# Writing out the batch loop, and reworking the first microseconds and the last stages, of a scan-mixer kernel

## The reference

```python
# mixer block, on u = layernorm(x)
logits  = u @ gate_W                          # 4 mixers, the best 2 per token are used
weights = softmax(top2(logits))
g, v, d = u @ Wg[m] + bg, u @ Wv[m] + bv, u @ Wd[m] + bd      # m = 0..3, each 256 -> 256
h[m]    = linear_scan(sigmoid(g) * tanh(v), 0.001 + 0.998 * sigmoid(d))   # along the 1024 tokens
a       = sum over the chosen m of weight[m] * h[m]
t       = x + layernorm(a)
# expert block, on z = layernorm(layernorm(t)) * ln_g + ln_b
e, gate = argmax and max of softmax(batchnorm(mean over tokens of z) @ Wr + br)   # one expert of 8 per sequence
y       = (relu(z @ W_down[e] + b_down[e]) @ W_up[e] + b_up[e]) * gate            # 256 -> 64 -> 256
out     = t + layernorm(y)
```

## Time and profile before

| | us |
|---|---|
| median of 3 runs (lowest, highest) | 683.45 (683.26, 683.74) |
| the profiled execution's own time | 683.75 |
| its span, from the first instruction to the last | 681.9 |
| PE (TensorE matmul) busy | 624.9, 92% |
| DVE (VectorE) busy | 595.3, 87% |
| ACT (ScalarE) busy | 432.1, 63% |
| POOL (GpSimd) busy | 162.8, 24% |

### The profile page before, as it was taken

The page is one execution under the profiler, slowest core; times in us unless marked ns, Lnnn a source line. Parts: engine busy times, 40 slices in busy tenths (PEclk is TensorE's granted clock), DMA queues, the critical chain, the costliest instruction groups (busy, mean ns, idle before and its releaser), DMA issues. The chain is left out here.

```text
span 681.9 us, 11013 instructions
## 1 busy us (share of the span) xinstructions
PE 624.9 (92%) x3457; PEld 331.8 (49%) x3457; DVE 595.3 (87%) x1289; ACT 432.1 (63%) x757; POOL 162.8 (24%) x238
## 2 busy tenths in 40 slices
PE   3999989999999999999999999999999999999132
PEld 1555445555545554555545554555545554554121
DVE  7593999979999899989999899989999889978976
ACT  2757746875578657775578657875678655776033
POOL 2006024101820065101820064102720051101111
PEclk9999998999999999999999999999999999999666
DMA  8800522030312113030313023030311010000003
GB/s 230 206 1 0 124 91 65 2 105 1 124 32 69 37 65 93 1 105 1 124 31 81 25 72 87 1 105 1 124 31 43 1 63 2 0 13 1 0 26 110
DMA packets 63702, 39.08 MB, mean 57 GB/s; under 512 B 34934, under 2 KB 63642, under 8 KB 63642
## 3 DMA queue, kind: packets, MB, share of 16 engines
q1 hardware_dynamic: 63644, 38.34, 20.3%
HBM read 21.03 MB, written 8.39 MB: 43 GB/s over the span
## 5 line engine op out<-in xcount | busy, mean ns | idle before, releaser
L1229 PE MATMUL ps_main<-x_feat,w_hi 128*128 128x512 f16 x1536 | 471.3, 381 | 2.4 <-ACT x_feat L541 1.5
L1229 PE MATMUL ps_main<-x_feat,w_lo 128*128 128x512 f16 x768 | 292.4, 381 | 0.0
L1229 PEld LDWEIGHTS ps_main<-x_feat,w_hi 128*128 128x128 f16 x1536 | 151.6, 99 | 179.8 <-issue 3.1
L837 DVE TENSOR_TENSOR_SCAN hid<-decay_s,value_s 128x1024 f32<-128x1024 f32 (+1 forms) x64 | 144.7, 2260 | 6.7 <-DVE value_s L857 1.7
L562 ACT ACTIVATE value_s<-ps_main,vecs 128x512 f32<-128x512 f32 x128 | 88.6, 692 | 90.0 <-PE ps_main L1229 89.9
L562 ACT ACTIVATE decay_s<-ps_main,vecs 128x512 f32<-128x512 f32 x128 | 88.6, 692 | 62.5 <-PE ps_main L1229 50.5
L1229 PEld LDWEIGHTS ps_main<-x_feat,w_lo 128*128 128x128 f16 x768 | 75.5, 98 | 83.8 <-issue 1.4
L562 ACT ACTIVATE gate_s<-ps_main,vecs 128x512 f32<-128x512 f32 x128 | 88.6, 692 | 42.0 <-PE ps_main L1229 39.8
L447 POOL TENSOR_TENSOR root_y<-root_in_y,neg_half 128x8 f32<-128x8 f32 (+1 forms) x9 | 18.8, 2091 | 292.1 <-DVE root_in_y L943 292.1
L850 DVE SCALAR_TENSOR_TENSOR mixed<-ps_aux,comb,mixed 128x256 f32<-128x256 f32 x192 | 77.2, 474 | 12.1 <-PE ps_aux L1239 9.9
L857 DVE TENSOR_TENSOR value_s<-gate_s,value_s 128x1024 f32<-128x1024 f32 (+1 forms) x66 | 78.3, 1187 | 5.7 <-ACT value_s L562 5.7
(11 more groups left out here) (158 smaller groups left out, 548.4 us busy)
## 6 DMA issues: line engine op xcount, KB each, us to landing
x_in<-in_L_attn_x SPq DMA_DIRECT2D x16, 512.0 KB, 4.4
resid<-in_L_attn_x SPq DMA_DIRECT2D x7, 1024.0 KB, 5.2
out<-resid SPq DMA_DIRECT2D x7, 1024.0 KB, 4.5
expert<-experts SPq DMA_DIRECT2D x8, 192.5 KB, 2.2
w_stage<-in_L_attn_Wg SPq DMA_DIRECT2D x4, 256.0 KB, 3.8
w_stage<-in_L_attn_Wd SPq DMA_DIRECT2D x4, 256.0 KB, 5.1
w_stage<-in_L_attn_Wv SPq DMA_DIRECT2D x4, 256.0 KB, 5.1
u_split<-in_L_ffn_W_down SPq DMA_DIRECT2D x4, 256.0 KB
```

What stands on the lines that cost most here:

```text
L837: dve.tensor_tensor_scan(states(pc), staged(decay_s, pc, pc.c), staged(value_s, pc, pc.c), start, ALU.mult, ALU.add).then_inc(scanned, 1)
L1229: ins = pe.matmul(ps_main[:, i % BANKS], w[:, 3 * m + kind, k, half * P:(half + 1) * P], feat(low, bt, k, c), start=(n == 0), stop=(n == 3 ...
```

## The change

Every engine's stream is written out: the `Fori` loops become Python loops, and semaphore increments that nobody waited for go (`plain_begun`, `turn_begun`, `index_seen`, `shift_begun`). TensorE's stream now begins with 45 transposes of the identity into a PSUM bank, whose result is never read. The first bank's six matmuls are reordered, high x first, and each waits for its own input. W_down is loaded once, in two DMAs instead of four, and `hidden_bias` takes two experts per matmul (eight instead of sixteen), whose sums VectorE adds in four pieces instead of one. In batch 7's last stages TensorE gets 16, 8, 15, 2 and 2 matmuls of 128x512 whose result is never read (`keep_awake`), `down` is replaced by `down_last` (six matmuls of 64 output rows per chunk instead of four of 128), `join_h` and `low_h` by `plain_h` with ScalarE on one side of chunk 1, and the last rows are shared: ScalarE scales 6 tiles, VectorE scales 2 and adds 6, GpSimd adds 2.

```diff
-            with eng.Fori(0, B // 2 - 1) as j:
+            for j in range(B // 2 - 1):
...
-            for k in range(KT):
-                for a in range(2):
-                    sp.dma_start(down_stage[:, :, k, a * H:(a + 1) * H],
-                                 W_down[:, k * P:(k + 1) * P, :].rearrange("e p h -> p e h")
-                                 ).then_inc(experts_loaded, 16)
+            for k in range(KT):
+                sp.dma_start(down_stage[:, k], W_down[:, k * P:(k + 1) * P, :].rearrange("e p h -> p e h")
+                             ).then_inc(experts_loaded, 16)
...
-                for part in range(2 * C):
-                    sp.wait_ge(out_ready, C * bt.n + part + 1)
+                for part, ready, count in ((0, early_out, 1), (1, out_ready, C * bt.n + 1), (3, own_out, 1),
+                                           (2, out_ready, C * bt.n + 2)):
+                    sp.wait_ge(ready, count)
...
+                rows = t_rows(bt)
+                for t in scalar_rows(0)[:T // C // 2]:
+                    pool.wait_ge(y_normed, T + t + 1)
+                    ins = pool.tensor_tensor(rows[:, t], y_rows[:, t], rows[:, t], ALU.add)
+                ins.then_inc(early_out, 1)
...
                 router_sigmoids(bt)
-                for c in range(C):
-                    hidden_part(bt, c)
-                    high_h(bt, c)
+                act.wait_ge(h_ready, done(bt, 0))
+                act.activation(up_in2[0:H, chunk(0)], h32[0:H, chunk(0)], ACT.Relu).then_inc(hp_ready, 1)
+                act.wait_ge(down_done, done(bt, 1))
+                act.activation(h32[0:H, chunk(1)], ps_aux[0:H, KT], ACT.Relu,
+                               bias=expert[0:H, HB:HB + 2].bitcast(F32), scale=Q_W * H_SCALE).then_inc(hh_ready, 1)
+                act.wait_ge(hh_ready, done(bt, 0))
+                act.activation(up_in1[0:H, chunk(1)], h32[0:H, chunk(1)], ACT.Copy).then_inc(hh_ready, 1)
+                act.activation(up_in2[0:H, chunk(1)], h32[0:H, chunk(1)], ACT.Copy).then_inc(hp_ready, 1)
                 for c in range(C):
                     act.wait_ge(y_scaled, B + c)
-                    scale_rows(tiles(c))
+                    scale_rows(scalar_rows(c))
...
+            def plain_h(b, c):
+                if c == 0:
+                    dve.wait_ge(down_done, done(b, c))
+                    dve.tensor_scalar(h32[0:H, chunk(c)], ps_aux[0:H, KT * c], Q_W * H_SCALE,
+                                      expert[0:H, HB:HB + 2].bitcast(F32), ALU.mult, ALU.add).then_inc(h_ready, 1)
+                    dve.wait_ge(h_ready, done(b, c))
+                    dve.tensor_scalar(up_in1[0:H, chunk(c)], h32[0:H, chunk(c)], 0.0, None, ALU.max
+                                      ).then_inc(h_rounded, 1)
+                    dve.wait_ge(h_rounded, 1)
+                else:
+                    dve.wait_ge(hh_ready, done(b, c))
+                dve.scalar_tensor_tensor(up_in1[H:P, chunk(c)], h32[0:H, chunk(c)], 0.0, up_in1[0:H, chunk(c)],
+                                         ALU.max, ALU.subtract).then_inc(up_in_ready, 1)
+            def finish_last(b):
+                rows = t_rows(b)
+                own = [t for t in tiles(1) if t not in scalar_rows(1)]
+                dve.wait_ge(y_scaled, b.n + C)
+                for t in own:
+                    dve.tensor_scalar(y_rows[:, t], ps_tok[:, t], mul_by["y"][:, t:t + 1], add_y[:, t:t + 1],
+                                      ALU.mult, ALU.add).then_inc(own_rows, 1)
+                for n, t in enumerate(scalar_rows(0)[T // C // 2:]):
+                    dve.wait_ge(y_normed, T + T // C // 2 + n + 1)
+                    ins = dve.tensor_tensor(rows[:, t], y_rows[:, t], rows[:, t], ALU.add)
+                ins.then_inc(out_ready, 1)
+                for n, t in enumerate(own):
+                    dve.wait_ge(own_rows, n + 1)
+                    ins = dve.tensor_tensor(rows[:, t], y_rows[:, t], rows[:, t], ALU.add)
+                ins.then_inc(own_out, 1)
+                for n, t in enumerate(scalar_rows(1)):
+                    dve.wait_ge(y_normed, T + T // C + n + 1)
+                    ins = dve.tensor_tensor(rows[:, t], y_rows[:, t], rows[:, t], ALU.add)
+                ins.then_inc(out_ready, 1)
...
+                early = first and pc.plane == 0 and kind == GATE
...
+                terms = [(k, w, low) for k in range(KT) for w, low in ((w_hi, 0), (w_lo, 0), (w_hi, 1))]
+                if early:
+                    terms.sort(key=lambda term: term[2])
+                for n, (k, w, low) in enumerate(terms):
+                    if early:
+                        pe.wait_ge(xl_ready if low else xh_ready, KT * c + k + 1)
...
+            for _ in range(45):
+                pe.transpose(ps_main[:, BANKS - 1, 0:P], ident[:], ident[:])
             turn_x(first, 0)
...
-                for e in range(E):
+                for q in range(E // 2):
                     for k in range(KT):
...
+            def keep_awake(n):
+                for _ in range(n):
+                    pe.matmul(ps_main[:, 0], w_hi[:, 0, 0, 0:P], feat(0, first, 0, 0), start=True, stop=True)
...
                     turn_h(bt, 3, c)
+                pe.wait_ge(main_read, EVAC * B)
+                pe.wait_ge(t_ready, done(bt))
+                keep_awake(16)
                 for c in range(C):
                     pe.wait_ge(combined, summed_up(bt, 3, c))
                     turn_u(bt, c)
+                keep_awake(8)
                 route(bt)
-                down(bt)
-                for c in range(C):
-                    up(bt, c)
+                keep_awake(15)
+                pe.wait_ge(ul_ready, KT * C * (bt.n + 1))
+                for c in range(C):
+                    down_last(bt, c)
+                keep_awake(2)
+                up(bt, 0)
+                keep_awake(2)
+                up(bt, 1)
```

More of the change, by code:

```diff
@@ L107, in mixer_kernel @@
         up_in2 = sb("up_in2", [P, S], F16)
[L109 to L110 removed]
+        down_stage = u_split[:].bitcast(F32).rearrange("p a k s -> p (a k s)")[:, 0:KT * E * H].rearrange(
+            "p (k e h) -> p k e h", k=KT, e=E)
         up_stage = resid[:, 0]
@@ L269, in state_tile, with scalar_rows @@
             return hid[:, (KT * m + k) % 4, t * P:(t + 1) * P]
+        def scalar_rows(c):
+            return tiles(c) if c == 0 else tiles(c)[:T // C // 2]
         y_rows = x_in[:, 0]
@@ L416, in _ @@
             load_resid(Batch(1, 1, False))
-            with sp.Fori(0, B // 2 - 2) as j:
+            for j in range(B // 2 - 2):
                 run(j, 1)
@@ L1018, in prepare_down @@
                 lo = experts[:, :, (2 * k + 1) * H:(2 * k + 2) * H]
-                w = down_stage[:, :, k, 0:H]
+                w = down_stage[:, k]
                 link(dve.tensor_scalar(hi, w, small[:, 5, k:k + 1], None, ALU.mult))
@@ L1043, in prepare_biases @@
                 dve.wait_ge(bias_turned, 1)
-                link(dve.tensor_tensor(r8[:, 0], ps_bias, vecs[:, B_DOWN:B_DOWN + E], ALU.add))
+                for into in (slice(0, H), slice(H, P)):
+                    sums = r8[into, 0].rearrange("p (q o) -> p q o", o=2)
+                    rows = vecs[into, B_DOWN:B_DOWN + E].rearrange("p (q o) -> p q o", o=2)
+                    dve.tensor_tensor(sums[:, :, 0], ps_bias[0:H], rows[:, :, 0], ALU.add)
+                    ins = dve.tensor_tensor(sums[:, :, 1], ps_bias[H:P], rows[:, :, 1], ALU.add)
+                link(ins)
                 dve.tensor_scalar(experts[:, :, HB:HB + 2].bitcast(F32).rearrange("p e a -> p (e a)"), r8[:, 0],
@@ L1167, in last @@
                 for c in range(C):
-                    join_h(bt, c)
-                    low_h(bt, c)
+                    plain_h(bt, c)
                 for c in range(C):
@@ L1215, in product @@
                 m, half = divmod(pc.plane, KT)
-                if first and pc.plane == 0 and kind == GATE:
-                    pe.wait_ge(xh_ready, KT * (c + 1))
-                    pe.wait_ge(xl_ready, KT * (c + 1))
+                early = first and pc.plane == 0 and kind == GATE
                 if i == 0 and not first:
@@ L1225, in product @@
                     pe.wait_ge(main_read, EVAC * bt.n + i - BANKS + 1)
-                n = 0
-                for k in range(KT):
-                    for w, low in ((w_hi, 0), (w_lo, 0), (w_hi, 1)):
-                        ins = pe.matmul(ps_main[:, i % BANKS], w[:, 3 * m + kind, k, half * P:(half + 1) * P],
-                                        feat(low, bt, k, c), start=(n == 0), stop=(n == 3 * KT - 1))
-                        n += 1
+                terms = [(k, w, low) for k in range(KT) for w, low in ((w_hi, 0), (w_lo, 0), (w_hi, 1))]
[4 more added lines that the diff above has]
+                        pe.wait_ge(xl_ready if low else xh_ready, KT * c + k + 1)
+                    ins = pe.matmul(ps_main[:, i % BANKS], w[:, 3 * m + kind, k, half * P:(half + 1) * P],
```

(12 more changed lines are left out.)

23 lines of the change are left out of this document (10 added, 13 removed).

## The result

The changed kernel takes 673.7 us (median of 4 runs, 672.99 to 674.89) against 683.6 us before on the same chip (4 runs, 683.26 to 684.0): a ratio of 0.9855 with a 95% interval of 0.984 to 0.987, so it is 1.5% faster, clear of the noise. The prediction was 673.0 us in a range of 669.8 to 678.4. The profiled execution is the slowest of the four: 674.89 us, with a span of 673.1 us; the other three have spans of 671.2 to 672.0 us. Its span is 8.8 us shorter than the 681.9 us of before.

A forecast was written before the change was run, and what follows sets the result against it. PE, busy for 92% of the span, was taken as the bound. Terms 1.4 + 1.75 + 1.7 + 2.2 + 3.4 = 10.4 us off 683.75 gave 673.3, and 673.0 us for the median; range 669.8 to 678.4.

The forecast's parts named there:

- What bounds the kernel: PE is the bound; time can be won only at the start, around `hidden_bias`, at loop returns and in the tail.
- The start: Before the first products: reordered bank 0 and transposes raising the clock let products go on earlier; 1.4 us, bounds 0 and 1.9.
- `hidden_bias`: In batch 0: half of its 32 passes saves 1.75 us, and the clock staying up behind them 1.7 us.
- Batch 1: DVE's lateness of 2.71 us and the clock falling behind that wait are not touched: 0, up to 2.1 us.
- The loop: Before batches 3 and 5: each return costs 1.08 us, two give 2.2 us; bounds 2.0 and 2.3.
- The tail: From `turn_u` to the end: `turn_u` at full clock, `plain_h` and a new row division win 3.4 us; bounds 1.5 and 4.0.
- The last rows ... Gain 0.2: End of the tail: with six rows for ACT, DVE is the limit at 4.0 us instead of 4.2; gain 0.2.
- The sum: All terms together: 10.4 us off the profiled execution's 683.75 us, 673.3; median of the runs 673.0 us.
- straight code: Rival: written-out batches 3 to 6 are fetched more slowly, 17.6 us dearer in all, 690.6 us; chance 0.05.
- DVE swallows the lead: Rival: in batch 0 DVE's work holds PE's banks back, only loop and tail remain, 5.6 us, 677.9 us; chance 0.12.
- Transposes don't count: Rival: at the start the 45 transposes stay slow and cost 2 us instead of giving 1.4; 676.4 us; chance 0.06.
- The clock falls at the wrong times: Rival: start gives 0, the second half of `hidden_bias`' gain is gone, tail gives 1.9; 5.9 us, 677.6 us; chance 0.20.

The follow-up runs named there:

- e2: The changed kernel without the 45 unread transposes at the start: 673.62 us, ratio 0.9858 to the kernel before.
- e4: The changed kernel with each of the eight `hidden_bias` matmuls issued twice, same sums, 32 passes as before the change: 675.29 us, ratio 0.987 to the kernel before.
- e3: The changed kernel without the 43 unread matmuls in the tail (`keep_awake` returns at once): 677.06 us, ratio 0.9899 to the kernel before.
- e8: The changed kernel with 52 unread transposes instead of 45, and further ones in PE's waits up to chunk 1's turn: 672.91 us, ratio 0.9838 to the kernel before.
- e1: The kernel before with only its two device loops written out: 681.26 us, ratio 0.9964 to the kernel before.
- e6: The changed kernel with GpSimd's two adds of the last rows done by DVE itself: 672.96 us, ratio 0.9838 to the kernel before.
- e0: The changed kernel once more, unaltered, on another chip: 674.12 us, ratio 0.9852 to the kernel before.
- e5: The changed kernel with GpSimd's two adds waiting until DVE has finished `scale_y`: 672.98 us, ratio 0.9836 to the kernel before.

## Why the prediction was right, step by step

- *What bounds the kernel* was right: nothing but the four places gave anything, and the loop's gain lay in its body too.
- *The start* (1.4 us) was too high: 0.5, near its lower bound. The step that failed is the choice between its bounds, "PE's last wait, before chunk 1's turn, is only about a microsecond". It was (0.84 us), but the clock had fallen before it, at 11.7 us, behind the wait of 1.61 us. The rest of the working held: transposes do raise the clock (45 in 6.75 us, which at 0.24 us each would be 10.8; first turn 1.09), against the sentence of the Trainium skill cited there, and bank 0 was done by 14. What the prediction missed is that without the transposes PE's own work would have brought the clock up in time (e2), since chunk 1's turn waits for DVE until 15 us either way. The transposes contributed nothing to the 0.5 us, even where the clock held.
- *`hidden_bias`* (1.75 + 1.7) was right to 0.5 us. The passes take 1.84 us, the clock stays at 1.00, and all of it reached the next batch: DVE still waits 7.41 us for PE, now before 63.33. The missing half microsecond is the additional pieces of the bias sum: from there to the wait in batch 1 DVE takes 35.24 us (to 98.57) instead of 34.78 (67.27 to 102.05), and `gates` waits 0.60 us for it. e4 adds that the 1.7 us are not there in every execution.
- *Batch 1* (0) was right: the wait (2.66) and the clock behind it (0.83) stayed. But whether the clock falls there is not certain: e3 and e8 have the same waits and 1.00, and the batch takes 79.0 us in both.
- *The loop* (2.2, at most 2.3) was too small: 3.0. The term counted returns only, and took a batch without one as the floor. Such a batch pays 0.17 us too (e1).
- *The tail* (3.4, bounds 1.5 to 4.0) gave 2.2. `turn_u` takes 1.94 us and ACT's last split comes 1.05 us earlier relative to it; `down` 1.1 us earlier; `plain_h` starts right behind the gate work, 1.9 us earlier (1.8 predicted); and from there to `y_moments` it takes 3.38 us (3.40 predicted). The term that failed is the last one, "The last rows ... Gain 0.2": it is a loss of 1.1, of which 0.9 lie before DVE's end and 0.2 behind it. I asked only whether GpSimd would be slow; at 0.7 us for an add it is not, as "at one microsecond each they are hidden" has it, but DVE's two small passes beside it are held up, which makes the 0.9. Undisturbed there would have been no gain either: e6's 4.89 us less its two further adds (0.67) leave 4.2, the time of before, because DVE starts 1.2 us behind ACT and takes 0.99 for its two passes from PSUM, where 1.1 and 0.8 had been put (an estimate from e6's rows).
- *The sum* is 1.6 us too high for the profiled execution (+0.8 for the loop, -0.9 for the start, -0.5 for `hidden_bias`, -1.2 for the tail, and 0.2 from stretches costed at nothing), which is the slowest of the four runs; against their median it is off by 0.7 us, or 0.1%. That closeness is in part luck: the loop's additional 0.8 us offset a part of the 2.6 us by which the other terms fell short, and the median is of executions some of which may have kept the clock where the profiled one lost it.

Of the rivals, *straight code* is refuted by e1 and by the even period. *DVE swallows the lead* is refuted by its 7.41 us. *Transposes don't count* is refuted by the first turn. *The clock falls at the wrong times* came true at the start alone. For the start, the wait behind the transposes goes with it (under e8); why one execution keeps the clock behind batch 1's waits and another loses it stays open. The spread of the changed kernel goes with it: e0's runs of 675.46 and 675.14 us have a mean granted clock of 0.975, its run of 672.27 us one of 0.981. At which stage an execution that wasn't profiled lost it isn't shown.

## What to carry to other kernels

Look at the seam between a warm-up and the steady state for an engine that is off the bound: here DVE idled for 7 us and then made PE wait half a batch later, and three calls moved into that gap were worth 5 us, more than any single part of the change. Fill a gap with unread work only if it lasts up to the work that counts; 43 matmuls in the tail were worth 3.2 us. The 45 transposes at the start were worth nothing: PE's own work has the clock up in time without them, and where the wait behind them is long the clock is lost again. When work is given to another engine, price what it does to its neighbour's passes and not only how long it takes.

## What the hardware showed that was not expected

- The device loop costs 0.17 us in each batch on PE beside the 1.1 us at each return (periods of 75.88 and 76.96 us against 75.71 in e1).
- GpSimd adding 128x256 float32 (0.7 us each) makes DVE's 128x4 passes with two SBUF inputs take 0.56 and 0.65 us instead of 0.16, and an add of 128x256 0.82 instead of 0.41 (e5); DVE's passes from PSUM beside it keep their time (0.99 for two).
- The same wait of 2.66 and 0.47 us was followed by a clock of 0.83 in the changed kernel, e0 and e4, and of 1.00 in e3 and e8.
